# Four long products on a constant tile ahead of the first matmuls, and the prologue's loads, bias products and exponentials in another order

## The reference, cut to what matters

```python
W = weights[condition]                        # one of 16 sets of 32x32 for each of 128 batch rows
h = einsum('bct,bcd->bdt', x, W)              # x: 128 x 32 x 512
q = (h @ Wq_c.T + bq_c) @ Wq_up.T + bq_up     # 32 heads, 128 + 64 columns each
kv = h @ Wkv_c.T + bkv_c                      # 64 latent columns, 64 of rope
k, v = split(kv[..., :64] @ Wkv_up.T + bkv_up)
x = x + softmax(q k^T / sqrt(192)) v @ Wo.T + bo      # 32 tokens, per batch row and head
taps = 2 * einsum(Cs, exp(dtA * arange(512))).real    # dtA = (-exp(log_A) + i A_imag) * exp(log_dt)
y = mask * (convolution of mask * x with taps + D * mask * x)
x = x + y @ dequantized(qweight).T + bias
```

## Time and profile before

| | |
|---|---|
| median of 3 runs | 803.2 us (802.5 to 806.75) |
| the profiled execution | 804.07 us, span 802.1 us |
| TensorE, matmul records | 764.8 us (95% of the span), x6833 |
| VectorE | 631.2 us (79%), x1107 |
| ScalarE | 417.7 us (52%), x748 |
| GpSimd | 277.1 us (35%), x261 |
| mean DMA rate | 70 GB/s |

### The profile page before, as it was taken

How to read it: one execution, slowest core, us unless ns; L and a number is a source line. 1 busy time by engine, 2 the same in 40 slices (tenths; PEclk the granted TensorE clock), 3 DMA queues, 4 the chain that set the end, 5 groups by cost and what they waited for, 6 DMA issues and landing times.

```text
span 802.1 us, 16920 instructions
## 1 busy us (share of the span) xinstructions
PE 764.8 (95%) x6833; PEld 641.8 (80%) x6833; DVE 631.2 (79%) x1107; ACT 417.7 (52%) x748; POOL 277.1 (35%) x261
## 2 busy tenths in 40 slices
PE   6999999999999998999999999999888799999996
PEld 6877788778788876877887888788766689999996
DVE  4567889998998695769677676957998678888887
ACT  1474737555573776465555837555565422332221
POOL 4001313040222229031311313020143487888871
PEclk9999999999999999999999999999999899999999
DMA  9911010210011020001301100202033538889861
GB/s 242 209 54 28 2 31 1 54 32 1 14 40 31 1 54 2 29 1 29 67 2 24 30 31 1 54 1 56 9 100 90 154 82 205 211 203 206 199 140 67
DMA packets 60093, 55.84 MB, mean 70 GB/s; under 512 B 24384, under 2 KB 46960, under 8 KB 60016
## 3 DMA queue, kind: packets, MB, share of 16 engines
q1 hardware_dynamic: 57744, 54.07, 27.4%
q0 software_dynamic: 1056, 0.49, 0.4%
q10 hardware_dynamic: 1216, 0.19, 0.2%
HBM read 41.91 MB, written 8.63 MB: 63 GB/s over the span
## 4 chain that ended last, share of the span: by engine, by line
PE 75%; DVE 18%; POOL 3%; ACT 2%; issue 2%; DMA 1%; DVEq 0%; ACTq 0%; POOLq 0%
PE ps L744 25%; PE ps L620 8%; PE ps L621 7%; PE ps L622 7%; PE ps L791 5%; DVE z_low L1480 4%; PE ps L636 4%; PE ps L1078 4%; PE ps L1079 4%; DVE sc L1469 2%; PE ps L1047 2%; PE ps L817 2%; PE ps L707 1%; DVE pT L1473 1%; DVE sc L1461 1%
## 5 line engine op out<-in xcount | busy, mean ns | idle before, releaser
L537 POOL TENSOR_TENSOR pT_low<-pT,pT_high 128x512 fp32r<-128x512 f32 x60 | 82.1, 1370 | 364.6 <-ACT pT_high L1195 364.6
L1181 ACT ACTIVATE qt<-ps,m_bias 128x512 f32<-128x512 f32 x242 | 155.1, 684 | 76.4 <-PE ps L744 74.7
L744 PE MATMUL ps<-q_high,m_high 64*128 64x512 f32 x768 | 153.5, 396 | 1.8 <-ACT qt L1181 1.3
L744 PE MATMUL ps<-q_high,m_low 64*128 64x512 f32 x768 | 150.3, 387 | 0.0
L744 PE MATMUL ps<-q_low,m_high 64*128 64x512 f32 x768 | 108.3, 387 | 0.0
L744 PEld LDWEIGHTS ps<-q_high,m_high 64*128 64x128 f32 x768 | 72.2, 184 | 24.7 <-issue 5.7
L1480 DVE TENSOR_TENSOR z_low<-ps,z_high 128x512 fp32r<-128x512 f32 x128 | 78.2, 682 | 8.2 <-ACT z_high L1211 8.2
L744 PEld LDWEIGHTS ps<-q_low,m_high 64*128 64x128 f32 x768 | 72.3, 184 | 15.1
L744 PEld LDWEIGHTS ps<-q_high,m_low 64*128 64x128 f32 x768 | 72.3, 184 | 13.9
L1186 ACT ACTIVATE sc<-sc 128x512 f32<-128x512 f32 x60 | 37.7, 631 | 64.1 <-DVE sc L1461 64.0
L1211 ACT CAST z_high<-ps 128x512 fp32r<-128x512 f32 x128 | 65.0, 618 | 7.8 <-PE ps L817 7.2
(11 more groups left out here) (296 smaller groups left out, 1829.0 us busy)
## 6 DMA issues: line engine op xcount, KB each, us to landing
x_in<-in_x SPq DMA_DIRECT2D x16, 512.0 KB, 4.4
x_s<-in_x SPq DMA_DIRECT2D x32, 256.0 KB, 5.6
out<-res SPq DMA_DIRECT2D x31, 256.0 KB, 3.1
toep_high<-taps_scratch SPq DMA_DIRECT2D x32, 192.0 KB, 4.4
toep_low<-taps_scratch SPq DMA_DIRECT2D x32, 192.0 KB, 5.2
c_tok<-ctok SPq DMA_DIRECT2D x64, 64.0 KB, 2.1
wq_nope<-in_L_attn_Wq_up SPq DMA_DIRECT2D x2, 1536.0 KB, 12.1
toep_far<-taps_scratch SPq DMA_DIRECT2D x32, 64.0 KB, 5.6
```

Of the source, the lines that this page charges most:

```text
L537: pool.tensor_tensor(flat(pT_low[:, n]), flat(pT[:, n]), f(flat(pT_high[:, n])), ALU.subtract).then_inc(s["pl_done"], 1)
L744: mm = pe.matmul(ps[:, FOLD_BANK[(j // 2) % 2] + e, :], weights[rows, (GH * g + j) // 2, c, :], moving[c][rows, :], start=start, stop=stop)
L1181: act.activation(qt[:, j, :], ps[:, FOLD_BANK[(j // 2) % 2] + j % 2, :], ACT.Identity, bias=m_bias[:, h:h + 1]).then_inc(s["qt_done"], 1)
```

## The change

VectorE fills a new tile busy (128 x 512) with ones. TensorE waits for it and multiplies it by itself four times, into bank BO, ahead of the first selection products; nobody reads the result. cond_w has a semaphore of its own, so that VectorE waits for cond_all alone. x_in[1] is loaded ahead of wk; the query weights come in three parts (8, 8 and 16 heads), the stores of zeros behind the first, wv behind the second. TensorE's bias products move behind the mixing. On VectorE the two parts of the exponentials move behind projected_ab(0), and the three copies of the biases behind the third wcT_low. The rest is as it was.

```diff
@@ -206,6 +206,7 @@
     zero = t("zero", [C, KPAD], at=qt_at + 15 * KB)
     cond_f = t("cond_f", [P, B // 4], at=qt_at + 13 * KB + 512)
     ones = t("ones", [NH, 1], at=zh_at + 3 * KB + 32)
+    busy = t("busy", [P, T], at=m_at + 40 * KB)
 
     small_at = [zh_at + 8 * KB]
 
@@ -306,6 +307,7 @@
     LATE_ZBANK = ((BO, BX), (BS, BS + 1), (BZ, BZ + 1), (BO, BX))
     LAST = NU - 1
     LAG = 3
+    BUSY = 4
     qt_count = lambda u, j: GH * u + j - max(0, min(u, LAST) - 1)
     f_bank = lambda c: 6 if c < C - 2 else 2 if c == C - 2 else 0
     flat = lambda ap: ap.rearrange("p b a n -> p (b a n)")
@@ -342,23 +344,24 @@
             sp.dma_start(wc_raw[64:P, 1, :], wq_c[0:64, :]).then_inc(s["wc_in"], 16)
             sp.dma_start(wc_raw[:, 2, :], wkv_c).then_inc(s["wc_in"], 16)
             sp.dma_start(x_in[0][:], x_v[:, 0:2, :]).then_inc(s["x_loaded"], 16)
+            sp.dma_start(x_in[1][:], x_v[:, 2:4, :]).then_inc(s["x1_loaded"], 16)
             wkv = d["L0_attn_Wkv_up"].rearrange("(h n) c -> n h c", h=NH)
             sp.dma_start(wk[:], wkv[0:NOPE]).then_inc(s["wk_in"], 16)
-            sp.dma_start(x_in[1][:], x_v[:, 2:4, :]).then_inc(s["x1_loaded"], 16)
             wq = d["L0_attn_Wq_up"].rearrange("(h n) c -> n h c", h=NH)
-            for n in range(2):
-                hs = slice(n * NH // 2, (n + 1) * NH // 2)
-                pairs = slice(n * NPAIR // 2, (n + 1) * NPAIR // 2)
-                arrived = (s["wq_in0"], s["wq_in1"])[n]
-                sp.dma_start(wq_nope[:, hs, 0:QL], wq[0:NOPE, hs]).then_inc(arrived, 16)
+
+            def load_queries(h0, h1, arrived):
+                sp.dma_start(wq_nope[:, h0:h1, 0:QL], wq[0:NOPE, h0:h1]).then_inc(arrived, 16)
                 for e in range(2):
-                    sp.dma_start(wq_rope[64 * e:64 * e + 64, pairs, :],
-                                 wq[NOPE:QH, n * NH // 2 + e:(n + 1) * NH // 2:2]).then_inc(arrived, 16)
-            sp.dma_start(wv[:], wkv[NOPE:NOPE + VH]).then_inc(s["wv_in"], 16)
-
+                    sp.dma_start(wq_rope[64 * e:64 * e + 64, h0 // 2:h1 // 2, :],
+                                 wq[NOPE:QH, h0 + e:h1:2]).then_inc(arrived, 16)
+
+            load_queries(0, NH // 4, s["wq_in0"])
             sp.wait_ge(s["zero_ready"], 1)
             for n in range(3):
                 sp.dma_start(scratch_taps[n][:, 0:KPAD], zero[:]).then_inc(s["taps_stored"], 16)
+            load_queries(NH // 4, NH // 2, s["wq_in1"])
+            sp.dma_start(wv[:], wkv[NOPE:NOPE + VH]).then_inc(s["wv_in"], 16)
+            load_queries(NH // 2, NH, s["wq_in2"])
 
             def load_x(i):
                 sp.wait_ge(s["h_ready"], 2 * i - 2)
@@ -674,8 +677,10 @@
                     pe.wait_ge(s["wq_in0"], 48)
                 if g == 1:
                     pe.wait_ge(s["q_done"], 2)
+                if g == QUADS // 4:
+                    pe.wait_ge(s["wq_in1"], 48)
                 if g == QUADS // 2:
-                    pe.wait_ge(s["wq_in1"], 48)
+                    pe.wait_ge(s["wq_in2"], 48)
                 if g == 0:
                     pe.wait_ge(s["bq_copied"], 1)
                     pe.wait_ge(s["bias_done"], 2)
@@ -924,7 +929,10 @@
                                        start=(k == 0), stop=(k == 3))
                     mm.then_inc(s["first_mix"], 1)
 
-            pe.wait_ge(s["cond_in"], 32)
+            pe.wait_ge(s["busy_ready"], 1)
+            for _ in range(BUSY):
+                pe.matmul(ps[:, BO, :], busy[:, 0:P], busy[:], start=True, stop=True)
+            pe.wait_ge(s["cond_w_in"], 16)
             first_mixing(0)
             pe.wait_ge(s["ident_ready"], 2)
             pe.wait_ge(s["wc_in"], 64)
@@ -933,15 +941,14 @@
                     mm = pe.transpose(ps[:, BS + m_, t_ * P:(t_ + 1) * P], wc_raw[:, m_, t_ * P:(t_ + 1) * P], ident[:])
                 mm.then_inc(s["wcT_ready"], 1)
             first_mixing(1)
+            mixed_x(0)
+            mixed_x(1)
             pe.wait_ge(s["bias_in"], 16 * 6)
             pe.wait_ge(s["const_ready"], 2)
             pe.transpose(ps[:, BO, 0:NH], bq_raw[:, 0:NOPE], ident[0:NH, 0:NH])
             pe.matmul(ps[64:P, BO, 64:64 + NH], bq_raw[:, NOPE:QH], ident[0:NH, 0:NH], start=True, stop=True)
             pe.matmul(ps[:, BO, 100:101], bkv_raw[:, NOPE:NOPE + VH], ones[:], start=True,
                       stop=True).then_inc(s["bias_ready"], 1)
-
-            mixed_x(0)
-            mixed_x(1)
             project_ca(0)
             project_ab(0)
             pe.wait_ge(s["wk_in"], 16)
@@ -1105,7 +1112,7 @@
         def _(act):
             col = lambda ap: ap.rearrange("(p a) -> p a", a=1)
             act.dma_start(cond_all[:], d["itok_B_0_15"].partition_broadcast(P)).then_inc(s["cond_in"], 16)
-            act.dma_start(cond_w[:], d["L0_cond_weights"].rearrange("(k s) c e -> (s c) k e", k=4)).then_inc(s["cond_in"], 16)
+            act.dma_start(cond_w[:], d["L0_cond_weights"].rearrange("(k s) c e -> (s c) k e", k=4)).then_inc(s["cond_w_in"], 16)
             act.dma_start(bq_raw[:], d["L0_attn_bq_up"].rearrange("(h n) -> h n", h=NH)).then_inc(s["bias_in"], 16)
             act.dma_start(bkv_raw[:], d["L0_attn_bkv_up"].rearrange("(h n) -> h n", h=NH)).then_inc(s["bias_in"], 16)
             act.dma_start(bq_c[:, 0:1], col(d["L0_attn_bq_c"][0:P])).then_inc(s["bias_in"], 16)
@@ -1535,7 +1542,8 @@
                 dve.tensor_copy(taps[:, 16 * n:16 * n + 16, :],
                                 ps[0:LA, BX, :].rearrange("a (h c) -> a h c", c=LC)).then_inc(s["taps_done"], 1)
 
-            dve.wait_ge(s["cond_in"], 32)
+            dve.memset(busy[:], 1.0).then_inc(s["busy_ready"], 1)
+            dve.wait_ge(s["cond_in"], 16)
             dve.wait_ge(s["delta_ready"], 8)
             for k in range(4):
                 dve.tensor_scalar(chosen[:, k, :], cond_all[:, 0:16], float(4 * k), set_of[:, 0:1], ALU.subtract,
@@ -1567,25 +1575,25 @@
             dve.wait_ge(s["cond_step"], 4)
             dve.wait_ge(s["const_ready"], 1)
             dve.tensor_scalar(row_of[:], cond_f[:], l_pos[:, 0:1], None, ALU.add).then_inc(s["row_ready"], 1)
-            dve.wait_ge(s["ssm_in"], 80)
-            exp_begun(dve, chain, log_in[:], ek[:], ep[:])
             first_weights(1)
             for m_ in range(2):
                 dve.wait_ge(s["wcT_high_done"], m_ + 1)
                 dve.tensor_tensor(wcT_low[:, :, m_, :], ps[:, BS + m_, :].rearrange("p (t n) -> p t n", t=TT),
                                   f(wcT_high[:, :, m_, :]), ALU.subtract).then_inc(s["wcT_done"], 1)
-            dve.wait_ge(s["bias_ready"], 1)
-            dve.tensor_copy(wq_nope[:, :, QL], ps[:, BO, 0:NH]).then_inc(s["bq_copied"], 1)
-            dve.tensor_copy(m_bias[64:P, :], ps[64:P, BO, 64:64 + NH]).then_inc(s["bias_done"], 1)
-            dve.tensor_copy(bv_sum[:], ps[:, BO, 100:101]).then_inc(s["bias_done"], 1)
             mixed_low(0)
             mixed_low(1)
             dve.wait_ge(s["wcT_high_done"], 3)
             dve.tensor_tensor(wcT_low[:, :, 2, :], ps[:, BS + 2, :].rearrange("p (t n) -> p t n", t=TT),
                               f(wcT_high[:, :, 2, :]), ALU.subtract).then_inc(s["wcT_done"], 1)
-            exp_ended(dve, chain, log_in[:], ek[:], ei[:], ep[:])
+            dve.wait_ge(s["bias_ready"], 1)
+            dve.tensor_copy(wq_nope[:, :, QL], ps[:, BO, 0:NH]).then_inc(s["bq_copied"], 1)
+            dve.tensor_copy(m_bias[64:P, :], ps[64:P, BO, 64:64 + NH]).then_inc(s["bias_done"], 1)
+            dve.tensor_copy(bv_sum[:], ps[:, BO, 100:101]).then_inc(s["bias_done"], 1)
             projected_ca(0)
             projected_ab(0)
+            dve.wait_ge(s["ssm_in"], 80)
+            exp_begun(dve, chain, log_in[:], ek[:], ep[:])
+            exp_ended(dve, chain, log_in[:], ek[:], ei[:], ep[:])
             bias_part(0)
             weights_low(0)
             bias_part(1)
```

More of the change, by code:

```diff
@@ L275, in build @@
     res = [t(f"res{n}", [B, T], at=(qt_at + (28 + 2 * n) * KB if n < 2 else m_at + 46 * KB)) for n in range(3)]
-    weight_names = ("wc_in wq_in0 wq_in1 wk_in wv_in bias_in cond_in ident_ready const_ready wcT_ready wcT_high_done "
+    weight_names = ("busy_ready cond_w_in wc_in wq_in0 wq_in1 wq_in2 wk_in wv_in bias_in cond_in ident_ready const_ready wcT_ready wcT_high_done "
                     "wcT_done lat_ready lat_done fold_ready fold_high fold_done wvT_ready wvT_high_done wvT_done "
```

## The result

The changed kernel took 799.41 us in the median of 6 executions (799.12 to 800.0), the kernel before 805.62 us (802.5 to 807.12, 6). The measured ratio, 0.9937 with a 95% interval of 0.9919 to 0.9956, is not the quotient of the two medians, which is 0.9923; by the ratio the changed kernel is 0.6% faster, by the medians 0.8% (6.2 us). The profiled execution took 799.7 us with a span of 797.6, 4.5 us less than before.

What follows compares the result with a forecast made beforehand. It took TensorE's unbroken prologue path, run at the lower clock, as the bound: 5.75 us gained at the projection less a 0.75 us standstill gives 5.0, so 799.1 us profiled or 798.2 against the median; range 796.5 to 802.1.

Steps and rivals of the forecast that it cites:

- The forecast: Whole kernel: 5.0 us gained, 799.1 us for the profiled execution, 798.2 against the median; chance 0.65.
- The long products: TensorE's start: they raise the clock, end at 7.4 us, lie in idle time and cost 0.15 us.
- A constant operand: Rival at the long products: a constant operand doesn't raise the clock; 804.8 us, chance 0.08.
- Records at the upper level: Prologue's selection, transposes and mixing: 134 ns per record at the upper clock level.
- cond_w's own semaphore: Ahead of the selection: chooser comes earlier, as VectorE waits for cond_all alone; no separate size given.
- The bias products: Behind the mixing: they fill the gap ahead of the projection, which starts at 18.3 instead of 24.06 us.
- The standstill ahead of products(2): TensorE waits there for bias_part(0), now behind the exponentials: 0.75 us lost.
- The loads: Reordered loads of x_in[1], queries and wv: all hidden behind other work.
- the early stores: First fold: they lift ScalarE's wait, which TensorE's path doesn't show; gain nothing.
- The clock falling back: Rival between long products and mixing: clock drops to the lower level again; 800.7 us, chance 0.20.
- upper price for it, 3.9 us: Upper bound on the loss if the clock falls back before the mixing: 3.9 us, giving 802.1 us.

Runs made afterwards that it cites:

- stores_last: Changed kernel with only the three small stores of zeros moved back behind all weight loads; 805.04 us, ratio 0.9987 to the kernel before.
- again: The changed kernel once more, no edit, on another chip; 805.51 us, ratio 0.9939 to the kernel before.
- only_long: Kernel before with only the memset and the four long products added; 809.16 us, ratio 0.9986 to the kernel before.
- again_2: The changed kernel unedited, measured on a further chip for comparison; 799.75 us, ratio 0.9918 to the kernel before.
- bias_ahead: Changed kernel with TensorE's bias products ahead of the mixing again; 801.30 us, ratio 0.9923 to the kernel before.
- bias_part_first: Changed kernel with bias_part(0) ahead of the exponentials on VectorE; 803.96 us, ratio 0.9931 to the kernel before; second run 798.43 us, 0.9903.
- old_loads: Changed kernel with all its loads in the old order, stores of zeros last; 802.10 us, ratio 0.9950 to the kernel before.
- old_exponentials: Changed kernel with the exponentials in their old two places on VectorE; 804.15 us, ratio 0.9965 to the kernel before.
- no_long: Changed kernel without its four long products (BUSY = 0); 808.81 us, ratio 0.9986 to the kernel before.
- long8: Changed kernel with eight long products instead of four; 803.06 us, ratio 0.9958 to the kernel before.

## Why the prediction was right

- **The forecast**, 5.0 us off the profiled execution and 0.62% off the median, met 4.5 us and 0.63%. The direction of each large step was as worked out, but three sizes were off and one edit was priced wrongly. At the first fold the gain was 5.9 us, not 5.0, and 1.4 us were lost again later; that the sum fits as well as it does is luck. The medians lie 6.2 us apart.
- **The long products** ended at 7.7 us (7.4 forecast). The selection began 0.5 us later than before, and the rest of them lay in idle time. Their eight records took 5.09 us (stores_last) to 6.71 us (again) between executions, which is how early or late the clock rose. A constant operand raised it in all ten profiles that had four, and with eight.
- **Records at the upper level** were mis-sized: 107 to 120 ns instead of 134, 8.65 us from the selection to the mixing's end instead of 10.2. The 134 were the mean of a stretch in which the clock was still rising (the earlier trace rows show a maximum of 421 ns in it). This gave 1.6 us more.
- **cond_w's own semaphore** brought nothing in this profile: cond_all landed so late that chosen started at 6.08 us instead of 5.72. In the eleven other profiles with it chosen started at 4.88 to 5.75 us, and in only_long, without it, at 6.47; so it may bring some tenths of a microsecond, which count only where the clock rises early and TensorE waits for chooser (0.53 us in again_2).
- **The bias products** filled the gap: no idle time ahead of L623 in the changed kernel, 0.60 us in bias_ahead. But bias_part_first, the same up to there, shows 0.68 us for h_low, and its second profile none; so the gap isn't always filled. The projection started at 17.17 instead of 18.3.
- **The standstill ahead of products(2)** was forecast at 0.75 us and is 0.70; it costs 0.94, as bias_part_first shows.
- **The loads** are the step that failed: the early stores, it said, "lift ScalarE's wait for them at the first fold, which TensorE's path doesn't show": nothing. That the queries are hidden was right. But the cover of the stores was the late fold. Before, ScalarE and TensorE show:

```profile
40.57 1.27 ACT L1181 ACTIVATE qt<-ps,m_bias 128x512 f32<-128x512 f32 x2 [1.64 <-DMA taps_scratch<-zero]
...
45.26 0.50 PE L744 MATMUL ps<-q_high,m_high 64*128 64x512 f32 x2
```

In old_loads and stores_last TensorE goes on 1.31 us after ScalarE has begun. By that the kernel before could have gone on at 41.9 us and came at 45.26: 3.4 us of cover. The changed kernel is there at 39.31, so stores that landed as before would have cost it an estimated 2.6 us. Measured are 1.25 us in old_loads, whose path is longer for want of x_in[1] and ahead of products(0), and 5.41 us, with the fall of the clock behind it, in stores_last, where they land later still (0.9987). The prediction charged nothing because it priced the new order, which is right, and did not ask what the old one would have cost.
- **The clock falling back** between the long products and the mixing was not seen in the three profiles of the changed kernel, though only selection products and transposes ran for 4.8 us. By the rule on transposes of the Trainium skill, "TensorE: Matmul & The Clock Gate" ("Part 4: PE-mode transpose"), the fall was likelier; here 1.3 us of them did not bring it. The fall did come in old_exponentials, behind 2.10 us without any product. In bias_ahead it came 0.5 us into the mixing, behind selection products, transposes and bias products, which is the place of this rival; what brought it there, and not in the others, is open. The prediction's upper price for it, 3.9 us, does not come out of its terms (1.3 + 1.0 + 1.4 is 3.7); nothing rests on that.
- **Lost later:** 1.4 us, by the fall of the clock in the unit before the last. No rival had it. In again_2 that fall was missing, and its lead over the profile before, 6.5 us up to the last scores, was still only 5.4 at the end: there the clock's fall of 6.8 us, which every profile has at a standstill of 4.1 us near 620 us, began behind that standstill and not within it.

The kernel before spreads over 5.6 to 6.6 us on each of the three chips, the changed one over 1.5 (again_2) and 4.0 (again). The one profile of the kernel before is of an execution of 804.07 us, below its median of 805.62. What its longer ones lose is open; a longer wait for the stores would be one cause, and was not tried. When the clock first rises in them would be another.

## What to carry to other kernels

An early stretch of small products may run at TensorE's lower clock without any sign in the granted clock: read the durations, and if the engine is idle before, fill that time with long products that nobody reads. When a path gets shorter, price the old cover of everything that it will meet earlier: a small store behind megabytes of loads was free before and would have eaten an estimated 2.6 us of the 5.9; put last in the new order, it ate nearly all. And put what frees an engine's buffer (here two tiny copies) ahead of a chain that nobody waits for yet.

## What was not expected of the hardware

The eight equal records of the long products took between 5.09 and 6.71 us from one execution to the next. One and the same standstill of 1.92 to 1.95 us, in the unit before the last, is in all 14 profiles; the granted clock fell behind it in four (the changed kernel's, again, no_long, old_loads) and held in the other ten, with and without long products on both sides. Six of those ten show falls of their own in the first 100 us: at 13.7 us (bias_ahead), 17.5 and 96 (old_exponentials), 42 (stores_last), 44 (only_long), 91 (bias_part_first) and 94 (long8). And the granted clock reads 1.00 over the first 21 us of the kernel before, in which each mixing record took 421 ns instead of 275.
